# Copying an attention group's output bank on VectorE instead of ScalarE, for seven of a batch's eight groups

## The reference

```
x = x + layernorm(attention(layernorm(x)))      # 16 heads of width 8, from the left half of the features
x = x + layernorm(ffn(layernorm(x)))            # 3 cycles of a small coupling network with gelus

energy = einsum('nqhd,nkhd->nqkh', q, k)        # q, k, v = left @ Wq.T, Wk.T, Wv.T
att    = softmax(energy / 4, axis=2)
out    = einsum('nqkh,nkhd->nqhd', att, v).reshape(N, S, 128) @ Wo.T + bo
```

## Time and profile before

| | |
|---|---|
| median of 3 runs | 3399.24 us (3398.83 to 3399.82) |
| span of the profiled execution, first to last instruction | 3391.6 us |
| mean granted clock of TensorE over the span | 0.985 |
| busy | PE 95%, DVE 88%, ACT 84%, POOL 26% |

### The profile page before, as it was taken

The page is one execution under the profiler, slowest core; times in us unless marked ns, Lnnn a source line. Parts: engine busy times, 40 slices in busy tenths (PEclk is TensorE's granted clock), DMA queues, the critical chain, the costliest instruction groups (busy, mean ns, idle before and its releaser), DMA issues.

```text
span 3391.6 us, 56526 instructions
## 1 busy us (share of the span) xinstructions
PE 3222.9 (95%) x19712; PEld 941.5 (28%) x19712; DVE 2992.7 (88%) x5577; ACT 2843.6 (84%) x3752; POOL 897.6 (26%) x1322
## 2 busy tenths in 40 slices
PE   6989999999999999999999999999999999999987
PEld 2222232322323232232322323232232322323223
DVE  7999989999898998989989898998989989898943
ACT  3868979798897979979798897979979798896975
POOL 5002050321505123050320505123050320504015
PEclk7998999999999999999999999999999999999999
DMA  3111111121111112121121111112121121111001
GB/s 90 26 41 43 32 50 33 44 50 44 50 31 51 43 39 55 33 61 32 44 49 44 50 31 51 42 39 55 33 61 32 45 49 44 38 32 51 8 22 38
DMA packets 97498, 144.75 MB, mean 43 GB/s; under 512 B 49472, under 2 KB 60096, under 8 KB 89408
## 3 DMA queue, kind: packets, MB, share of 16 engines
q1 hardware_dynamic: 93520, 123.83, 13.8%
q0 software_dynamic: 3696, 17.31, 2.8%
HBM read 34.61 MB, written 32.51 MB: 20 GB/s over the span
## 4 chain that ended last, share of the span: by engine, by line
PE 67%; DVE 17%; ACT 8%; issue 3%; SPq 2%; DMA 1%; POOL 1%; DVEq 0%; POOLq 0%; ACTq 0%
PE heads_ps L514 24%; PE ring_ps L481 15%; DVE max_parts L966 12%; PE scoresT_ps L499 11%; PE scoresT_ps L602 7%; ACT p_sb L719 4%; DVE stats L977 3%; PE scoresT_ps L607 2%; ACT headsT L728 1%; PE ring_ps L543 1%; SPq L346 1%; DVE state L1030 1%; ACT state L784 1%; DVE moments L987 1%; PE ring_ps L529 1%
## 5 line engine op out<-in xcount | busy, mean ns | idle before, releaser
L966 DVE TENSOR_REDUCE max_parts<-ring_ps 128x1 f32<-128x512 f32 x3744 | 2369.2, 683 | 225.4 <-PE ring_ps L481 166.3
L719 ACT ACTIVATE p_sb<-scoresT_ps 128x1024 f32<-128x1024 f32 x2048 | 1970.1, 1024 | 81.4 <-PE scoresT_ps L499 57.7
L481 PE MATMUL ring_ps<-k_rows,q_rows 48*128 48x512 bf16 x3744 | 1086.0, 384 | 33.1 <-DVE max_parts L966 23.8
L514 PE MATMUL heads_ps<-p_sb,v_sb 128*9 128x512 f32 x8192 | 1071.4, 595 | 17.9 <-ACT headsT L728 11.9
L499 PE MATMUL scoresT_ps<-q_rows,k_rows 51*128 51x512 bf16 x4096 | 1021.3, 383 | 7.1 <-ACT p_sb L719 4.3
L481 PEld LDWEIGHTS ring_ps<-k_rows,q_rows 48*128 48x128 bf16 x3744 | 265.5, 94 | 1353.4 <-DVE max_parts L966 1242.4
L1233 POOL CAST max_wide<-max_all 128x16 bf16<-128x16 f32 x128 | 25.4, 198 | 1743.0 <-DVE max_all L972 1743.0
L602 PE MATMUL scoresT_ps<-state,w 128*128 128x512 f32 x732 | 364.9, 621 | 13.3 <-DVE state L1030 12.3
L824 ACT ACTIVATE p_sb<-scoresT_ps,b 128x512 f32<-128x512 f32 x180 | 123.8, 688 | 194.2 <-PE scoresT_ps L602 193.2
L499 PEld LDWEIGHTS scoresT_ps<-q_rows,k_rows 51*128 51x128 bf16 x4096 | 207.0, 93 | 224.4 <-ACT p_sb L719 211.5
L514 PEld LDWEIGHTS heads_ps<-p_sb,v_sb 128*9 128x9 f32 x8192 | 124.4, 88 | 288.8 <-issue 278.3
(11 more groups left out here) (196 smaller groups left out, 2635.9 us busy)
## 6 DMA issues: line engine op xcount, KB each, us to landing
q_rows<-parts SPq DMA_DIRECT2D x744, 32.0 KB
k_rows<-parts SPq DMA_DIRECT2D x744, 32.0 KB
x_sb<-in_x SPq DMA_DIRECT2D x16, 1024.0 KB, 4.8
x_in<-in_x SPq DMA_DIRECT2D x15, 1024.0 KB, 5.4
out<-x_sb SPq DMA_DIRECT2D x15, 1024.0 KB, 3.9
out<-x_in POOLq DMA_DIRECT2D x15, 1024.0 KB, 7.9
q_rows<-max_rows SPq DMA_DIRECT2D x512, 3.0 KB
feat_h<-headsT SPq DMA_DIRECT2D x512, 16.0 KB
```

What stands on the lines that cost most here:

```text
L481: e.matmul(ring_bank(max_taken, u + 1), q_rows[rows, slot, pair, h * BANK + qb * P:h * BANK + (qb + 1) * P], k_rows[rows, slot, pair, kh * ...
L514: m = e.matmul(heads_ps[32 * j:32 * j + DH + 1, :], v_sb[:, b % 2, kb, 4 * (group % NG) + j, 0:DH + 1], p_sb[:, n % 2, j, :], start=(kb == ...
L719: e.activation(p_sb[:, n % 2, 2 * two:2 * two + 2, :].rearrange("p h n -> p (h n)"), scoresT_ps[:, (2 - 2 * two) * BANK:(4 - 2 * two) * BA ...
L966: e.tensor_reduce(max_parts[:, gi % 2, kh, col:col + 1], bank_of(max_taken, u + 1), AX.X, ALU.max).then_inc(max_taken, 1)
```

## The change

ScalarE no longer copies `heads_ps` for the first seven groups of a batch; it keeps the last group's copy (`take_last_heads`). VectorE makes the seven copies with `tensor_copy`, in the opening step, behind the reduces of the units ahead of `weigh` (b and c; in batch 0 b, c and d) and in front of the reduce of unit a. The waits are the same two (`pv_done`, `heads_laid`). The orders of PE, SP and GpSimd are unchanged.

```diff
-            def take_heads(b, n):
-                group = n // NT
-                e.wait_ge(pv_done, step_of(b, n) + 1)
+            def take_last_heads(b):
+                e.wait_ge(pv_done, step_of(b, STEPS))
                 if b:
                     e.wait_ge(heads_laid, LAID * b)
-                e.activation(headsT[:, group // NG, group % NG, :], heads_ps[:, :], ACT.Copy).then_inc(heads_evac, 1)
+                e.wait_ge(heads_evac, GROUPS * (b + 1) - 1)
+                e.activation(headsT[:, NH - 1, NG - 1, :], heads_ps[:, :], ACT.Copy).then_inc(heads_evac, 1)
...
                     for two in range(2):
                         if valid(b):
                             exp(b, n, two)
-                    if valid(b) and n and n % NT == 0:
-                        take_heads(b, n - 1)
                 if valid(b):
-                    take_heads(b, STEPS - 1)
+                    take_last_heads(b)
...
+            def take_heads(b, group):
+                e.wait_ge(pv_done, step_of(b, NT * (group + 1)))
+                if b:
+                    e.wait_ge(heads_laid, LAID * b)
+                e.tensor_copy(headsT[:, group // NG, group % NG, :], heads_ps[:, :]).then_inc(heads_evac, 1)
...
                 for n in range(STEPS):
+                    upto = units_in_step(b, n, 1)
+                    max_units(done, upto)
+                    done = max(done, upto)
+                    if valid(b) and n and n % NT == 0:
+                        take_heads(b, n // NT - 1)
                     upto = units_in_step(b, n, 2)
                     max_units(done, upto)
                     done = max(done, upto)
```

## The result

| | before | after |
|---|---|---|
| median (lowest to highest), 18 runs each | 3398.95 us (3393.04 to 3418.17) | 3410.83 us (3405.32 to 3417.39) |
| ratio | | 1.0033, 95% interval 1.0026 to 1.0040 |
| profiled execution: span, mean granted clock | 3391.6 us, 0.985 | 3409.3 us, 0.981 |
| time of the profiled execution | not given | 3411.13 us |

The changed kernel is slower by 11.9 us, 0.33%. The forecast was 3410.8 us for the kernel and 11.6 us for the difference. That the time agrees to a tenth of a microsecond is luck: single runs of the changed kernel differ by 12 us, and the prediction's terms add up to about one microsecond more than the traces show (see the account behind the experiments).

What follows compares the result with a forecast made beforehand. Three nearly equal chains (PE, ScalarE, VectorE) bound each step; ScalarE's copy cost 0.28 us per opening, and the wait would move to VectorE. 8.1 + 3.7 - 0.2 = 11.6 us on 3399.24 gives 3410.8 us, range 3402 to 3420.

Steps and rivals of the forecast that it cites:

- The copy's duration: VectorE's 512-column copy, one per opening: occupies its queue for 0.60 us, 0.68 until PE is told, as the reduce.
- c late by 0.3 and `weigh` 0.54 behind it: Two steps behind the opening's unit c: c waits 0.3 us more for VectorE, and `weigh` follows it by 0.54.
- The plain opening as a draw: Opening step without a join: VectorE's lateness costs 0.30 us in place of ScalarE's 0.28, taken as 0.025 more.
- The joined opening: Openings 16 and 48, join ahead of b and c: 0.20 us formerly hidden now delays PE, 0.225 more each.
- Batch 0: Four units a step: unit a's reduce 0.53 us late at each of seven openings, nothing comes back, 3.7 us.
- The sum over a batch: Batches 1 to 14: 5 x 0.025 + 2 x 0.225 = 0.58 us each, 8.1 us for fourteen.
- The whole sum: All batches: 8.1 + 3.7 - 0.2 = 11.6 us slower.
- batch 15: Last batch: four plain openings and one joined lose 0.33 us; openings 48 and 56 return up to 0.28 each; together -0.2.
- that 7.6 us lie outside the first and last instruction: Before the change: median 3399.24 us is 7.6 more than the 3391.6 span, placed outside the first and last instruction.
- the kept gain: First rival: ScalarE's gain of 0.28 us per plain opening is kept if the copy is short; 3377 us, chance 0.11.
- No change: Rival: `weigh` follows c closer than 0.54, or copy occupies 0.50 to 0.55; within 0.2%, 3402 us, chance 0.14.
- a larger loss: Rival: copy occupies up to 0.69 us, or VectorE is told later of `pv_done`; 3421 us, chance 0.13.

## Why the prediction held, step by step

- **The copy's duration: right.** 0.68 with the next reduce 0.60 behind its start, x112, as the reduce on the same bank. The Trainium skill (VectorE: DVE Perf Modes, the TRN2 errata) gives by its formula an estimate of 0.66 us, near the 0.68 of the row. The Trainium skill (VectorE: DVE Perf Modes, Why PSUM operands drop a tier) allows fp32 from PSUM the single rate only, by an estimate with that page's 0.96 GHz 0.27 us for 256 columns. The rows agree: 0.41 for 256 columns and 0.68 for 512.
- **c late by 0.3 and `weigh` 0.54 behind it: right.** 2.74 and 3.28 from unit a where 2.75 and 3.29 stood; c to `weigh` is 0.54 in the plain opening (961.18, 961.72), and 0.53 in the step of the late c.
- **The plain opening as a draw: right.** 4.25 (predicted 4.26, before 4.24), and the kernel with mostly plain openings on VectorE measures 0.9997 of before. Over whole groups a plain opening loses 0.01 to 0.02, a little less than the 0.025 that stood.
- **The joined opening: right.** Unit a to unit a over the two steps, at opening 16, is 946.54 - 942.07 = 4.47, predicted 4.46:

```profile
942.07 0.09 PEld L481 LDWEIGHTS ring_ps<-k_rows,q_rows 48*128 48x128 bf16 x1 [0.86 <-DVE max_parts L964]
...
946.54 0.09 PEld L481 LDWEIGHTS ring_ps<-k_rows,q_rows 48*128 48x128 bf16 x1 [0.86 <-DVE max_parts L964]
```

- **Batch 0: right.** 2.99 where 3.00 stood, 0.52 to 0.53 more in each of the seven groups, 3.7 us in all as predicted; 3.2 to 3.5 us by medians at like clock.
- **The sum over a batch: right.** The copies of openings 8 and 56 of batch 4 start at 926.13 and 1023.61, 97.48 apart. Before it was 914.26 and 1011.22 (the second is in the earlier trace rows), 96.96. These six groups hold nearly all of the batch's loss: 0.52, where 0.58 stood for all seven. The first row below is before, the others after.

```profile
914.26 0.60 ACT L728 ACTIVATE headsT<-heads_ps 128x512 f32<-128x512 f32 x1
...
926.13 0.68 DVE L977 COPY headsT<-heads_ps 128x512 f32<-128x512 f32 x1
...
1023.61 0.68 DVE L977 COPY headsT<-heads_ps 128x512 f32<-128x512 f32 x1
```

- **The whole sum, from the traces: 10.7 us, where 11.6 stood.** I counted from the first exponential of one group to that of the next (for the group from 56, to the last exponential), at places with the same clock in both traces:

| per group, us | before | after | more | predicted |
|---|---|---|---|---|
| plain opening | 16.14 | 16.15 | 0.01 to 0.02 | 0.025 |
| joined opening | 16.14 | 16.37 | 0.23 | 0.225 |
| opening in batch 0 | 19.87 | 20.39 | 0.52 to 0.53 | 0.53 |
| batch 15, group from 48 | 15.40 | 15.03 | -0.37 | up to -0.28 |
| batch 15, group from 56 | 14.49 | 14.04 | -0.45 | up to -0.28 |

  A batch from 1 to 14 comes to 0.54, fourteen to 7.6; batch 0 adds 3.7 and batch 15 -0.5. So the plain openings and batch 15 were each put a little too dear. Why more than 0.28 comes back in batch 15's last two groups wasn't followed.
- **How the loss divides between the medians: joins 8.3, batch 0 5.1, the rest -1.5 us** (3405.73 - 3397.42, 3410.83 - 3405.73, 3397.42 - 3398.91), where 6.5 (29 x 0.225), 3.7 and 1.4 (the remainder of 11.6) stood. The deviations are of the size by which medians of differently clocked runs differ, so they correct no term; the table above does.
- **Wrong: that 7.6 us lie outside the first and last instruction.** The profiled execution of after has a time of 3411.13 and a span of 3409.3, 1.8 apart, and every other run has 1.76 to 1.95 between them. The other 5.8 were the profiled execution of before running at a clock of 0.985, where the median of its kind is 3393 us. It did no harm to the time, since I made the sum as a difference, but the forecast of the span, 3403, missed the 3409.3 by 6.
- **Mine and wrong, in the experiments:** that c can be moved behind `weigh`. The walk of the prediction followed PE to `weigh` and stopped; the next c's wait for the reduce of the last one, which it had used one step earlier, I left out there.

Of the rivals, the kept gain needs a copy that occupies less than 0.50, and the copy occupies 0.60. No change would have needed c closer to `weigh` than 0.54, and the trace shows the 0.54. For a larger loss the copy would have had to start late for `pv_done`; it starts without idle time. (In the first rival's sum batch 15 gives back 1.8 and not 1.9, which changes nothing.)

What I can't settle: the medians at like clock say only 7 to 11 us, since few runs stand at each clock and the mean clock is rounded to three places, of which one is worth about 3 us. The 10.7 of the traces rests on one execution of each kernel, though the same differences recur in batch after batch.

## What to carry to other kernels

Where three engines hand each other banks in nearly equal chains, moving an operation to the other engine moves the wait; walk the step with the new operation in its queue, up to the next one that reads the same bank, before trusting the idle time that the page shows. The page's line for the moved operation (11.9 us here) was neither the gain to be had nor the cost: on the engine that lost it, it hid 0.28 us an opening, and on the one that got it, the spare was 0.3 and the copy 0.6. Look for the few places where the taking engine has something else in the same slot (the joins, the fourth unit of batch 0): there nearly the whole loss was, and leaving those alone made the change neutral.

## What the runs showed of the hardware

- **The half clock lasts differently from run to run.** The kernel before with the join moved (shown) and the one with the joined openings on ScalarE both have 78 matmuls at a clock of 0.52 from 280 to 300, unlike the profiled execution of before (1.00), though all three run the same instructions in this stage:

```profile
280.00:300.00 20.00, 19.20 (x78) 0.52 0.22 69
```

  Over all runs of the kernel before beside the experiments the medians go from 3404.0 us at a mean clock of 0.981 (4 runs) to 3393.1 at 0.985 (6 runs): 11 us, as much as the change costs. The changed kernel's mean clock was 0.980 or 0.981 in 8 of 18 runs, before's 0.981 in 4 of 46. Whether the shifted timing of the changed kernel makes the longer half clock likelier wasn't tried.
- **A small operation directly behind its producer on VectorE** puts the next operation off by 0.22 us, one unit later by 0.08, for the same 128x16 tensor_tensor (941.30 - 940.48 less the usual 0.60, and 940.83 - 940.75).
- **A copy of 8 columns lasts 0.15, of 256 0.41, of 512 0.68 us** on VectorE from PSUM, and occupies its queue for 0.07, 0.33 and 0.60, each time 0.08 less than it lasts.
